# Reordered statistics, turns and rows of maxima in a two-layer decoder kernel

## The reference

```
x += mamba0(ln(x))      # selective scan, 512 channels x 16 states
x += xattn0(ln(x), ctx) # 16 heads of 64, l2-normed q and k, no softmax; then an MLP
x += ffn0(ln(x))        # first mixture
x += mamba1(ln(x))
x += xattn1(ln(x), ctx) # second cross attention
x += ffn1(ln(x))        # second mixture, top 2 of 8, and a shared expert
```

## Time and profile before

| | |
|---|---|
| median of 3 runs | 2972.07 us (2971.61 to 2978.2) |
| the profiled execution | 2965.96 us, span 2964.2 us |
| mean granted TensorE clock | 0.903 of full speed |
| TensorE busy | 2423.3 us, 82% of the span |
| VectorE busy | 2196.2 us, 74% |
| ScalarE busy | 1443.9 us, 49% |
| GpSimd busy | 893.1 us, 30% |
| first mixture, experts | 1315 to 1584 us |
| second cross attention | 2168 to 2539 us |

### The profile page before, as it was taken

The page is one execution under the profiler, slowest core; times in us unless marked ns, Lnnn a source line. Parts: engine busy times, 40 slices in busy tenths (PEclk is TensorE's granted clock), DMA queues, the critical chain, the costliest instruction groups (busy, mean ns, idle before and its releaser), DMA issues.

```text
span 2964.2 us, 31542 instructions
## 1 busy us (share of the span) xinstructions
PE 2423.3 (82%) x10888; PEld 1578.0 (53%) x10888; DVE 2196.2 (74%) x3180; ACT 1443.9 (49%) x2547; POOL 893.1 (30%) x617
## 2 busy tenths in 40 slices
PE   4979886588998899937992698888667879799998
PEld 1333332367776566737882234343233434789998
DVE  5999999698985564337886599999955643567776
ACT  5666474255664222215653665656402435347774
POOL 2868776200000000020002377777601223200004
PEclk7999999899998899968996799999987876889999
DMA  4032130570000000022421312303056241246652
GB/s 168 1 114 77 38 115 0 176 245 1 23 1 1 34 1 1 0 105 96 148 82 43 137 37 78 114 2 114 0 138 123 53 94 48 85 149 216 218 204 90
DMA packets 100067, 249.58 MB, mean 84 GB/s; under 512 B 9426, under 2 KB 63583, under 8 KB 91960
## 3 DMA queue, kind: packets, MB, share of 16 engines
q1 hardware_dynamic: 83540, 222.64, 23.3%
q0 software_dynamic: 4608, 12.59, 1.3%
q10 hardware_dynamic: 11760, 12.32, 1.3%
HBM read 194.42 MB, written 53.10 MB: 84 GB/s over the span
## 4 chain that ended last, share of the span: by engine, by line
PE 46%; DVE 28%; ACT 11%; issue 8%; DMA 3%; POOL 2%; ACTq 1%; SPq 0%; DVEq 0%; POOLq 0%
DVE psum L635 10%; PE psum L432 6%; PE psum L109 5%; PE psum L111 5%; PE psum L110 5%; PE psum L116 3%; DVE ch L643 3%; PE psum L397 3%; ACT WH L3101 2%; ACT g L3248 2%; PE psum L1265 2%; PE psum L1279 2%; PE psum L1249 2%; PE psum L1227 1%; PE psum L2535 1%
## 5 line engine op out<-in xcount | busy, mean ns | idle before, releaser
L317 POOL TENSOR_TENSOR bu<-u,row 128x1024 f32<-128x1024 f32 x254 | 597.2, 2356 | 289.0 <-DVE psum L635 189.8
L432 PE MATMUL psum<-ch,ident 128*128 128x512 f32 x1024 | 510.2, 627 | 139.9 <-DVE ch L643 139.4
L635 DVE TENSOR_TENSOR_SCAN psum<-psum,bu 128x1024 f32<-128x1024 f32 x256 | 585.5, 2287 | 18.9 <-ACT psum L514 18.7
L432 PEld LDWEIGHTS psum<-ch,ident 128*128 128x128 f32 x1024 | 187.7, 196 | 428.8 <-DVE ch L643 247.6
L514 ACT ACTIVATE psum<-dt,A 128x511 f32<-128x511 f32 x512 | 332.4, 682 | 0.4
L643 DVE TENSOR_TENSOR ch<-psum,row 128x1024 f32<-128x1024 f32 x256 | 312.8, 1222 | 7.6
L1535 POOL IOTA i<- 128x128 f32 x1 | 0.3, 345 | 710.3 <-DVEq L3393 710.3
L397 PE MATMUL psum<-hT,inw 128*128 128x512 f32 x256 | 138.2, 672 | 43.4 <-ACT sz L474 27.3
L3248 ACT ACTIVATE g<-psum,bias 128x256 f32<-128x256 f32 x248 | 101.1, 470 | 130.8 <-PE psum L111 126.8
L109 PE MATMUL psum<-WH,hs 128*128 128x256 f32 x496 | 144.9, 292 | 4.8 <-DVE hs L3328 2.3
L109 PE MATMUL psum<-xT,WH 128*128 128x256 f32 x496 | 141.0, 284 | 7.6 <-DVE xT L3291 7.6
(11 more groups left out here) (403 smaller groups left out, 5888.1 us busy)
## 6 DMA issues: line engine op xcount, KB each, us to landing
W<-in_m1W SPq DMA_DIRECT2D x24, 2052.0 KB, 8.6
row<-Ascr SPq DMA_DIRECT2D x64, 512.0 KB, 4.7
row<-Bscr SPq DMA_DIRECT2D x64, 512.0 KB, 4.8
m1buf<-zt SPq DMA_DIRECT2D x8, 2048.0 KB, 16.7
W<-in_m0W SPq DMA_DIRECT2D x16, 1024.0 KB, 5.2
WH<-x1scr SPq DMA_DIRECT2D x16, 384.0 KB, 8.1
x1scr<-hi SPq DMA_DIRECT2D x48, 128.0 KB, 2.4
qk<-x1scr SPq DMA_DIRECT2D x16, 384.0 KB, 8.4
```

Source lines behind the costliest of these rows:

```text
L317: e.tensor_tensor(m.bu[i % 3][:, :, :], u, m.row[:, g, 0, :, :], ALU.mult).then_inc(*m.fed.up)
L432: p = pe.matmul(m.y, k.ident, m.ch[i % RING_C][:, j, :], start=False, stop=g == UNITS - 1 and j == 1)
L635: dve.tensor_tensor_scan(flat, flat, m.bu[i % 3][:, :, :].rearrange("p a n -> p (a n)"), 0.0, ALU.mult, ALU.add).then_inc(*m.scan.up)
```

## The change

In the first mixture the statistics of a tile become a step of their own behind its addition, so `hidden` has eight steps instead of five. The additional steps are taken behind the subtractions of o = 1, 3 and 5, and the last one behind `columns(e + 2)`; at the start the last statistics come behind `first_split(1)`. In the last expert the output products of column o-1 stand behind the turns of column o and accumulate in banks 4 to 7, one for each t, instead of following all turns in the ring's banks.

In the second cross attention the maxima and the ones go from one tile to the other in one transfer each, without memory between. For batches 2 and 3 `x1_max_sp` comes ahead of the queries' spill and the loads, behind the keys' spill. The units of the last batch's period end by slot 15 instead of 22. The scatters of batches 0 and 1 move to slots 0 to 3 and 8 to 11 of the period two later, and those of batch 2 to slots 17 to 20 and 24 to 27 of the last. The change's title also names an order of the keys; no line of the diff touches another stage.

```diff
--- before.py
+++ after.py
@@ -1842,6 +1842,17 @@
     p.then_inc(*m.c_at.up)
 
 
+def last_out_pe(k, m, pe, e, o):
+
+    if o == 0:
+        pe.wait_ge(*m.W2l(2 * e + 1))
+    pe.wait_ge(*m.hl(8 * e + o))
+    for t in range(4):
+        p = mm3(pe, k.psum[:, 4 + t, 0:D], [h[:, o, 128 * t:128 * t + 128] for h in m.hs], [w[:, o, :] for w in m.W2s], o == 0, o == 7)
+        if o == 7:
+            p.then_inc(*m.o_at.up)
+
+
 def experts_pe(k, m, pe):
     own = Banks(m.banks4)
     bank = own.bank(pe)
@@ -1867,7 +1878,12 @@
                 p = turn_in(k, pe, bank[:, 128 * t:128 * t + 128], m.hN[e % 2][:, t, 128 * o:128 * o + 128])
             p.then_inc(*m.ht.up)
             own.freed_by(m.gelu(8 * e + o))
+            if e + 1 == E and o:
+                last_out_pe(k, m, pe, e, o - 1)
         step(rows)
+        if e + 1 == E:
+            last_out_pe(k, m, pe, e, 7)
+            break
         if e + 2 < E:
             columns_pe(k, m, pe, own, e + 2)
         pe.wait_ge(*m.W2l(2 * e + 1))
@@ -1938,9 +1954,9 @@
             hidden_norm(e + 1)
         if e + 2 < E:
             first_split(e + 2)
-        for t in range(4):
-            own.use()
         if e + 1 < E:
+            for t in range(4):
+                own.use()
             second_split(e + 1)
         act.wait_ge(*m.o_in(4 * e + 3))
         act.dma_start(k.DR["m0res"][CAP * e:CAP * e + CAP, :].rearrange("(t p) c -> p t c", p=128), m.ob[e % 2][:, :, :]) \
@@ -2001,12 +2017,12 @@
             dve.tensor_tensor(hN[:, t, :].rearrange("p (a n) -> p a n", a=2), m.h[n % 2],
                               m.b1[e % 2][:, :].rearrange("p (a n) -> p a n", a=2), ALU.add).then_inc(*m.hb.up)
             yield
-        for t in range(4):
-            dve.wait_ge(*m.hb(4 * e + t))
+            dve.wait_ge(*m.hb(n))
             for j in range(2):
                 s = dve.bn_stats(st[:, t, 6 * j:6 * j + 6], hN[:, t, 512 * j:512 * j + 512])
-        s.then_inc(*m.h_st.up)
-        yield
+            if t == 3:
+                s.then_inc(*m.h_st.up)
+            yield
 
     def hidden_norm(e):
         hN, st, mv = m.hN[e % 2], m.hst[e % 2], m.hmv[e % 2]
@@ -2059,10 +2075,12 @@
     first_split(0)
     second_split(0)
     columns(0)
-    for _ in hidden(0):
-        pass
+    rows = hidden(0)
+    for _ in range(7):
+        step(rows)
     columns(1)
     first_split(1)
+    step(rows)
     hidden_norm(0)
     for e in range(E):
         rows = hidden(e + 1) if e + 1 < E else iter(())
@@ -2078,9 +2096,11 @@
                 dve.wait_ge(*m.o_at(4 * (e - 1) + 3))
             dve.wait_ge(*m.hh(n))
             dve.tensor_tensor(m.hs[1][:, o, :], m.g[n % 3], m.hs[0][:, o, :], ALU.subtract).then_inc(*m.hl.up)
-        step(rows)
+            if e and o in (1, 3, 5):
+                step(rows)
         if e + 2 < E:
             columns(e + 2)
+        step(rows)
         if e + 1 < E:
             hidden_norm(e + 1)
         if e + 2 < E:
@@ -2089,7 +2109,7 @@
         if e >= 2:
             dve.wait_ge(*m.stored[e % 2](e // 2 - 1))
         for t in range(4):
-            bank = own.use()
+            bank = own.use() if e + 1 < E else k.psum[:, 4 + t, :]
             dve.wait_ge(*m.o_at(4 * e + t))
             dve.tensor_tensor(m.ob[e % 2][:, t, :], bank[:, 0:D], m.b2[e % 2][:, :], ALU.add).then_inc(*m.o_in.up)
         if e + 1 < E:
@@ -2316,7 +2336,7 @@
 X1_ALL = X1_LEAD + [u for p in X1_PERIODS for u in p if u != PAUSE] + x1_end(B - 1)
 X1_HIGH = {u: n for n, u in enumerate(u for u in X1_ALL if u[0] in "kq")}
 X1_AT = {u: n for n, u in enumerate(X1_ALL)}
-X1_LAST = [28, 28, 28, 22]
+X1_LAST = [28, 28, 28, 15]
 
 
 def x1_by_act(u):
@@ -2338,9 +2358,8 @@
 X1_SPLITS = [20, 22, 24, 26]
 
 
-X1_SENT = {(b + 1, 28 + i): (b, i) for b in range(2) for i in range(4)}
-X1_SENT.update({(b + 2, i): (b, 4 + i) for b in range(2) for i in range(4)})
-X1_SENT.update({(B - 1, 24 + i): (B - 2, i) for i in range(8)})
+X1_SENT = {(b + 2, 8 * (i // 4) + i % 4): (b, i) for b in range(2) for i in range(8)}
+X1_SENT.update({(B - 1, 17 + 7 * (i // 4) + i % 4): (B - 2, i) for i in range(8)})
 
 
 def x1_unit(u):
@@ -2370,12 +2389,11 @@
     m.one8, m.mf = m.oN[0:8, 0, :], m.oN[:, 1, 0:128]
     m.oT = al([128, 2, T], "oT")
     m.scr = k.dram("x1scr", [B, 2, 2, 48, 8, T])
-    m.scm, m.sc1 = k.dram("x1max", [B, 16, T]), k.dram("x1one", [8, T])
     m.st = [k.psum[:, 3:5, :], k.psum[:, 5:7, :]]
     m.ob = k.psum[:, 7, :]
     m.w_in, m.vecs = [c("x1w" + n, 1, 16) for n in "kqvo"], c("x1rows_of_all", 2, 16)
     m.mf_in, m.masks = c("x1mask_f", 2), c("x1masks", 1)
-    m.ones_in, m.ones_out, m.row_in = c("x1ones", 4), c("x1ones_out", 1, 16), c("x1ones_row", 4, 16)
+    m.ones_in, m.row_in = c("x1ones", 4), c("x1ones_row", 4, 16)
     m.ctx_in = [c(f"x1context{i}", 2, 16) for i in range(2)]
     m.fn_in = c("x1normed", NT)
     n_act = sum(x1_by_act(u) for u in X1_ALL)
@@ -2383,7 +2401,7 @@
     m.hi_in = c("x1high", 4 * B)
     m.spill = [[c(f"x1spill_{w}{j}", 6 * B, 16) for j in range(2)] for w in "kq"]
     m.loaded = [[c(f"x1loaded{i}{g}", 4 * 2, 16) for g in range(2)] for i in range(2)]
-    m.mx_out, m.mx_in = c("x1max_out", B, 16), c("x1max_in", 2 * B, 16)
+    m.mx_in = c("x1max_in", 2 * B, 16)
     m.sc, m.ex, m.cut = c("x1scores", 32 * B), c("x1exp", 32 * B), c("x1cut", 32 * B)
     m.pvs = c("x1weighted", 16 * B)
     m.on = c("x1group", 4 * B)
@@ -2592,7 +2610,7 @@
     elif w == "m":
         act.wait_ge(*m.full(n))
         if b:
-            act.wait_ge(*m.mx_out(b - 1))
+            act.wait_ge(*m.mx_in(2 * b - 1))
         act.copy(m.mx[:, :], bank[0:16, :]).then_inc(*m.by_act.up)
     elif w == "o":
         act.wait_ge(*m.full(n))
@@ -2764,24 +2782,20 @@
 
 def x1_max_sp(k, m, sp, b):
     sp.wait_ge(*x1_drawn(m, ("m", b, 0)))
-    sp.dma_start(m.scm[b], m.mx[:, :].bitcast(F32)).then_inc(*m.mx_out.up)
-    sp.wait_ge(*m.mx_out(b))
     if b >= 2:
         sp.wait_ge(*m.sc(32 * (b - 2) + 31))
     for i in range(2):
         sp.dma_start(m.q[b % 2][64 * i + 48:64 * i + 49, :, :].rearrange("p g t -> p (g t)").bitcast(F32),
-                     m.scm[b, 8 * i:8 * i + 8, :].rearrange("(o g) t -> o (g t)", o=1)).then_inc(*m.mx_in.up)
+                     m.mx[8 * i:8 * i + 8, :].bitcast(F32)).then_inc(*m.mx_in.up)
 
 
 def x1_ones_sp(k, m, sp):
 
     sp.wait_ge(*m.ones_in(3))
-    sp.dma_start(m.sc1, m.one8).then_inc(*m.ones_out.up)
-    sp.wait_ge(*m.ones_out(0))
     for i in range(4):
         o = 64 * (i % 2) + 48
         sp.dma_start(m.kk[i // 2][o:o + 1, :, :].rearrange("p g t -> p (g t)").bitcast(F32),
-                     m.sc1.rearrange("(o g) t -> o (g t)", o=1)).then_inc(*m.row_in.up)
+                     m.one8).then_inc(*m.row_in.up)
 
 
 def x1_context_sp(k, m, sp, b):
@@ -2815,10 +2829,13 @@
         if b + 2 < B:
             x1_context_sp(k, m, sp, b + 2)
             x1_spill_sp(k, m, sp, "k", b + 2)
+        if b and b + 1 < B:
+            x1_max_sp(k, m, sp, b + 1)
+        if b + 2 < B:
             x1_spill_sp(k, m, sp, "q", b + 2)
             x1_load_sp(k, m, sp, b + 2, 0)
-        if b + 1 < B:
-            x1_max_sp(k, m, sp, b + 1)
+        if b == 0:
+            x1_max_sp(k, m, sp, 1)
         if b + 2 < B:
             x1_load_sp(k, m, sp, b + 2, 1)
 
```

## The result

The changed kernel takes 2936.99 us (median of 4 runs, 2934.05 to 2939.53); the kernel before took 2971.84 us beside it (median of 4). The ratio is 0.9884, 95% interval 0.9864 to 0.9905: 35 us or 1.2% faster. The profiled execution took 2934.05 us (span 2932.3 us, clock 0.907), 31.9 us less than that of before.

A forecast was written before the change was run, and what follows sets the result against it. No one engine was taken to bound the whole; TensorE mostly sets the first mixture's pace. Terms summed to 31.3 us off the profiled 2965.96, so 2934.7, or 2941 us on the runs' median scale; range 2924 to 2957.

The forecast's parts named there:

- steady experts: First mixture, experts 1 to 5: statistics between subtractions remove TensorE's waits of 1.86 and 0.80 us; 2.66 us each, 13.3 us.
- start, the wait alone: First mixture's start: with statistics moved, TensorE's 8.64 us wait ends 4.3 us earlier; bounds 3 and 6.8 us.
- first expert, from the end of that wait: First mixture, first expert: ScalarE bounds it, so the gelu's 2.18 us wait goes; 2.2 us, bounds 0 and 4.
- last expert: First mixture's last expert: products between turns gain 3.1 us, half clock takes 1.8 us back; 1.3 us gained.
- first batch's row: Second cross attention, first batch: loads no longer wait for the store of the row of maxima; 1.6 us.
- third batch: Second cross attention, third batch: row of maxima lands before TensorE comes, loads then limit; 4.3 us, bounds 3.0 and 10.7.
- scatters, end of the third batch: Second cross attention, end of third batch: the second batch's scatters leave it; 1.8 us gained.
- last batch: Second cross attention, last four slots: scatters leave, 3.3 us, less 0.8 us of waiting; 2.5 us, bounds 1 and 4.2.
- The rival with VectorE as the bound: First mixture: VectorE bounds the turns, a steady expert gains only about 0.6 us, kernel takes 2951 us; chance 0.17.
- The clock's term: Last expert's products: 3.5 us at 1.2 GHz costs half of that, taking 1.8 us back from the overlap's gain.
- The rival of two experts at half clock: First mixture: two experts more than now run at half clock, kernel takes 2995 us; chance of slower by half clock 0.05.
- the weak ends: Low bounds together: 1.0 us per expert, 3 us lost in the last, 3.0 for third batch; leave 16 us, 2956.

The follow-up runs named there:

- The kernel with two columns: Changed kernel with the last expert's output products two columns behind the turns instead of one: 2953.62 us, ratio 0.991 to the kernel before.
- the experts-only kernel: Kernel before with only the first mixture's expert functions as after the change, second cross attention as before: 2945.88 us, ratio 0.9924.
- the attention alone: Kernel before with only the second cross attention's functions as after the change, first mixture as before: 2962.48 us, ratio 0.9978.
- the kernel through memory: Changed kernel with the rows of maxima through memory again at the new queue place, ones still direct: 2952.48 us, ratio 0.9905 to the kernel before.

## Why the prediction came out as it did

Predicted 2941 us in a range of 2924 to 2957, measured 2937. By its own terms:

| term | predicted, us | measured, us |
|---|---|---|
| steady experts | 13.3 | 16.3 |
| start, the wait alone | 4.3 | 4.1 |
| first expert, from the end of that wait | 2.2 | 2.3 |
| last expert | 1.3 | -0.1 |
| first batch's row | 1.6 | 1.6 in one pair of traces, 0.6 of it in the issue |
| third batch | 4.3 | 1.9 |
| scatters, end of the third batch | 1.8 | 1.6 |
| last batch | 2.5 | 0.5 |

**Steady experts.** Right in mechanism, too small: 3.3 us each, not 2.66, near the upper bound of 3.4. I had taken off the two waits as the timeline prints them. A wait costs more than that, because the idle time starts only at the modelled end of the last matmul, and the next ones start slowly. TensorE around both waits, before the change:

```profile
1492.25 0.28 PE L111 MATMUL psum<-W2s,hs 128*128 128x256 f32 x1
1494.39 0.38 PE L109 MATMUL psum<-W2s,hs 128*128 128x256 f32 x1 [1.86 <-DVE xs L1991]
1494.61 0.28 PE L110 MATMUL psum<-W2s,hs 128*128 128x256 f32 x1
...
1500.12 0.28 PE L111 MATMUL psum<-W2s,hs 128*128 128x256 f32 x1
1501.19 0.47 PE L109 MATMUL psum<-W1s,xs 128*128 128x512 f32 x1 [0.80 <-issue]
1501.50 0.40 PE L110 MATMUL psum<-W1s,xs 128*128 128x512 f32 x1
```

Without a wait a matmul of 256 columns starts 0.12 us behind the one ahead of it, and one of 512 columns 0.23 us. From start to start the first wait costs 2.02 us and 0.10 us at the next matmul, the second 0.95 and 0.08 us: 3.15 us. The last three of the five experts came 3.08 to 3.11 us closer (30.03 to 26.93 us). TensorE's busy time before would not have helped: 27.38 us of 30.03 leaves the same 2.65 us. The first two gained more, 3.40 and 3.57 us. The clock is at most a part of this: before the change the first and the fifth had 0.94, the others 1.00, and after it all have 1.00. The rival with VectorE as the bound was not far off: VectorE has 1.8 us left of 26.9.

**Start and first expert.** As worked out: the wait went from 8.64 to 4.57 us. From the first subtraction ScalarE's gelu and cast follow one another every 1.33 us without the wait of 2.18 us. (The experts' first product started 0.3 us later in the trace after the change, so expert 0's last addition is 6.1 us earlier and not 6.4.)

**Last expert.** The failed step is that the loop goes round every 1.9 us. With one column in flight a column's turns stand on TensorE behind products that wait for a subtraction, and its gelu, cast and subtraction only begin then: 2.19 us a column; two columns in flight made it 1.87. The clock's term was right: TensorE idled 4.95 us before its first product, whose matmuls then took 0.41 us each and 0.28 from 1545.7 on, and 1.2 GHz lasted 3.4 us (granted clock 0.51) where I had taken 3.5. The kernel with two columns had these too and took 2.7 us less than the kernel before, so the loop was what I lacked.

**First batch.** Right in sum and in part by luck. The step "the loads no longer wait for the store: 1.6 us" left out the price of the direct row's issue, 1.4 us for two against 0.5: the loads go out 0.6 us earlier. The rest of the 1.6 us lies within the spread of their landing.

**Third batch.** The failed step is "in a pause in which SyncE waits for the queries, so nothing queued behind is pushed back". SyncE's timeline after the change:

```profile
2355.78 1.24 SPq L2422 DMA_DIRECT2D x1scr<-lo  x2
2357.12 1.39 SPq L2788 DMA_DIRECT2D WH<-mx  x2
2358.55 1.14 SPq L2422 DMA_DIRECT2D x1scr<-lo  x2
2359.74 2.52 SPq L2422 DMA_DIRECT2D x1scr<-hi  x4
...
2366.22 4.35 SPq L2780 DMA_DIRECT2D qk<-x1scr  x8
```

Before the change the same place looked so:

```profile
2377.30 2.37 SPq L2404 DMA_DIRECT2D x1scr<-hi  x4
2379.71 2.95 SPq L2404 DMA_DIRECT2D x1scr<-lo  x4
```

The pause was the 0.6 us by which the second four spills take longer than the first. The row's two issues take 1.4 us, so from the first of these spills to the first load it takes 12.85 us instead of 11.91. The maxima then start 11.7 us after the first load is issued, where I had 11.0. Counted from a wait that both kernels have in the batch before (3.14 us, at 2349.99 and 2325.30 us), the loads are issued 1.7 us later than in the kernel before: 0.9 us by the row, and 0.8 us that arose ahead of these spills, for which I have no cause. 4.3 - 1.7 - 0.7 = 1.9 us, as measured between this pair. In the other kernels the landing alone differs by more than a microsecond, and counted from the products of the queries the gain is 2.1 to 3.7 us.

TensorE's wait for the loads is 10.84 us and not the 8 us that I looked for, but 2.5 us of it are no loss: the last weighted sum of the second batch had waited 2.53 us for its cut behind the scatters, and no longer does.

**Last batch.** The failed step is that scatters cost only where they stand between the last cuts. In a row of four a scatter with its cut takes 1.55 to 1.72 us, and three of the eight took 2.4 or 2.5 us, while slots 17 to 31 come every 1.2 us on average where the scatters are spread out. That puts GpSimd behind wherever the four stand, and TensorE waited 2.43 and 0.91 us. The 0.8 us of waiting for VectorE's ranks, which I had counted against the change, is there (0.8 us). The 0.5 us that remain in the table are not the change's either. The last batch before it:

```profile
2474.02:2527.33 53.31, 45.65 (x246) 21.43 (x244) 17.31 (x52) 29.55 (x46) 27.49 (x44) 0.63 0.18 65
```

TensorE's idle time rose from 7.7 to 8.8 us, and its busy time fell from 45.7 to 44.0 us with the clock (0.63 to 0.65). With the scatters at their old places the experts-only kernel took 51.0 us, at 0.67. Spreading them out is worth 2.3 us at the same clock.

**The clock.** The terms measured make 28.2 us, the profiled execution gained 31.9. Between them stand changes of the granted clock, up in the fourth stretch (0.71 to 0.82) and at the stage's end (0.67 to 0.98), and down in the second mixture. Windows there, 50 us that begin 50 us after its start, before and after:

```profile
2588.80:2638.80 50.00, 43.99 (x269) 37.46 (x268) 28.31 (x44) 18.21 (x32) 0.00 (x0) 0.80 0.32 111
```

```profile
2553.30:2603.30 50.00, 44.06 (x245) 36.71 (x244) 25.67 (x40) 15.72 (x29) 0.00 (x0) 0.73 0.30 107
```

It fell from 0.80 to 0.73 with the same code, which got through 245 matmuls in as much busy time as 269 before, and the mixture took 3.7 us more. A full or nearly full clock at the stage's end went with a longer mixture elsewhere too: on the two later chips it took 436.8 and 436.2 us in the kernels with spread scatters, whose stage ends at 0.70 and 0.71, and 441.8 to 442.8 us in the six others, which end at 0.76 to 0.97. In the experts-only kernel the stage ends at 0.69 and the mixture takes 426.8 us. That the one causes the other was not tried. The rival of two experts at half clock found nothing: the granted clock is 1.00 in all steady experts.

By the two halves the sum stands: the experts alone gave 22.6 us (18 to 27) where I had 21.1, the attention alone 6.5 us (2.4 to 10.7) where I had 10.2. That the total came within 4 us owes something to luck, in errors that cancel: the steady experts and the clock brought 7 us more than I had, the last expert, the third and the last batch 6 us less. One sum of the range was also off: the weak ends that it names leave 17.4 us, not 16, which gives 2955 for 2956 and changes nothing here.

## What to carry to other kernels

Count what a wait costs from the start of the last instruction ahead of it to the next start at the usual pace: here 3.1 us an expert, for 2.66 us of idle time. On a queue, look at what stands directly ahead of and behind the place to which an issue is moved: a pause has to be seen in that queue's own timeline and be longer than the issue, and a small transfer behind four large ones lands with them. A transfer that saves a way through memory can give a part of it back by a dearer issue. Before a stage of a single trace is called faster, compare TensorE's idle time there and not only the length, since the same code ran at another clock in the next execution. For a loop over several engines count how many items are in flight: one more column gave what the overlap was meant to give.

## What the runs showed of the hardware that I had not expected

The landing of a 16 KB row between two tiles went from at most 2.3 us with no load ahead to 6.72 us behind four loads of 384 KB each. Issuing such a row took 0.7 us, against 0.26 us for one from memory (0.52 for two, also in the kernel through memory).

The same program had granted clocks of 0.82 and 0.76, or 0.98 and 0.77, in the same stretch of two executions. The second mixture took 425.4 to 429.1 us in six profiles (before, after, and the four kernels run beside the median of 2968.8 us) and 436.2 to 442.8 us in the eight on the two other chips, where the kernel before was 10 and 17 us slower too.
